# A graph attention kernel: a bank stretch set to zero by VectorE instead of by a product of zeros, and eleven unread products per layer taken out

## The reference

```python
xw = x @ W
xj = xw[src].reshape(-1, H, D) + edge_emb.reshape(-1, H, D)
alpha = einsum(xi, att_i) + einsum(xj, att_j)
alpha = leaky_relu(alpha, 0.2)
ea = exp(alpha - segment_max(alpha, dst)[dst])
alpha = ea / (segment_sum(ea, dst)[dst] + EPS)
aggr = segment_sum(xj * alpha[..., None], dst)
h = aggr.mean(axis=1) + b        # relu between the layers
```

## Time and profile before

| | us |
|---|---|
| median of three runs | 3877.42 |
| the three runs | 3877.04, 3877.42, 3886.52 |
| the profiled execution's own time | 3864.76 |
| its span, first to last instruction | 3862.7 |

### The profile page before, as it was taken

How to read it: one execution, slowest core, us unless ns; L and a number is a source line. 1 busy time by engine, 2 the same in 40 slices (tenths; PEclk the granted TensorE clock), 3 DMA queues, 4 the chain that set the end, 5 groups by cost and what they waited for, 6 DMA issues and landing times.

```text
span 3862.7 us, 48694 instructions
## 1 busy us (share of the span) xinstructions
PE 2537.2 (66%) x13702; PEld 2037.0 (53%) x13702; DVE 2037.4 (53%) x6415; ACT 700.5 (18%) x3102; POOL 2210.4 (57%) x2357
## 2 busy tenths in 40 slices
PE   7778726666592767659276765927676592767669
PEld 6668615555471555546165554716555471655556
DVE  8966635555462555546255554625454462555546
ACT  0067521111121111112111111221111122111111
POOL 0066566666626766661676666167676616766661
PEclk8555555555565555556555555665555566555556
DMA  3212022222202222220222222022222202222221
GB/s 105 87 58 78 18 61 51 52 52 57 51 19 50 54 52 52 56 48 18 49 54 50 54 57 50 18 49 54 50 54 57 50 18 49 54 50 54 52 47 34
DMA packets 114123, 195.78 MB, mean 51 GB/s; under 512 B 39897, under 2 KB 77272, under 8 KB 113864
## 3 DMA queue, kind: packets, MB, share of 16 engines
q0 software_dynamic: 62560, 130.25, 14.9%
q1 hardware_dynamic: 51304, 62.42, 5.1%
HBM read 180.86 MB, written 11.67 MB: 50 GB/s over the span
## 4 chain that ended last, share of the span: by engine, by line
PE 32%; DVE 32%; another core or an unknown queue 18%; issue 14%; DVEq 3%; ACT 1%; ACTq 1%; POOL 0%; DMA 0%; POOLq 0%
PE bank L736 13%; PE bank L738 7%; DVE acc L1200 3%; PE bank L744 3%; PE bank L709 2%; PE bank L732 2%; DVEq L1018 2%; DVE alpha L1094 2%; PE bank L781 2%; DVE pw L1161 2%; DVE into L1143 2%; PE bank L762 1%; DVE prod L1072 1%; DVE ring L849 1%
## 5 line engine op out<-in xcount | busy, mean ns | idle before, releaser
L509 POOL DMA_INDIRECT ring<-table,srci x1955 | 1937.5, 991 | 937.9 <-issue 556.7
L736 PE MATMUL bank<-pw,ring 128*128 128x48 f32 x3910 | 1216.1, 405 | 181.9 <-issue 179.7
L736 PEld LDWEIGHTS bank<-pw,ring 128*128 128x128 f32 x3910 | 1016.8, 315 | 330.9 <-issue 258.5
L1200 DVE TENSOR_TENSOR acc<-acc,bank 128x288 f32 x490 | 222.8, 455 | 1215.5 <-remote 830.0
L738 PE MATMUL bank<-onehot,est 128*36 128x24 f32 x3910 | 631.1, 243 | 203.5 <-issue 202.8
L732 PE MATMUL bank<-zeros 128*128 128x288 bf16 x490 | 210.6, 430 | 726.2 <-DVE pw L1161 485.5
L738 PEld LDWEIGHTS bank<-onehot,est 128*36 128x36 f32 x3910 | 390.8, 149 | 369.3 <-issue 200.5
L732 PEld LDWEIGHTS bank<-zeros 128*128 128x128 bf16 x490 | 58.4, 119 | 802.5 <-DVE pw L1161 501.2
L579 ACT COPY ai_win<-ai_rows 128x48 f32 x1955 | 339.5, 229 | 472.1 <-issue 436.8
L585 ACT ACTIVATE dd<-dd 128x66 f32<-128x66 f32 x75 | 19.4, 259 | 2171.5 <-DVE dd L1154 975.7
L516 POOL TENSOR_TENSOR S<-S 128x128 f32<-128x128 f32 x125 | 61.1, 489 | 399.8 <-ACT S L589 393.9
(11 more groups left out here) (213 smaller groups left out, 2773.0 us busy)
## 6 DMA issues: line engine op xcount, KB each, us to landing
ring<-table,srci POOLq DMA_INDIRECT x1955
ai_rows<-lo_dram SPq DMA_DIRECT2D x28, 896.0 KB, 4.3
at<-in_attr SPq DMA_DIRECT2D x65, 224.0 KB
table<-ring SPq DMA_DIRECT2D x15, 390.0 KB, 3.7
table<-ring SPq DMA_DIRECT2D x5, 325.0 KB, 3.2
result<-ring SPq DMA_DIRECT2D x24, 64.0 KB
x_mid<-ring SPq DMA_DIRECT2D x3, 384.0 KB, 2.7
table<-ring SPq DMA_DIRECT2D x5, 130.0 KB, 2.3
```

The source lines that it names most:

```text
L509: nc.gpsimd.indirect_dma_start(out=ring[:, slot(t), :], out_offset=None, in_=table, in_offset=bass.IndirectOffsetOnAxis(ap=srci[:, t:t + 1 ...
L736: nc.tensor.matmul(wide[:, 0:H, at_k], ring[:, slot(t), 0:D], pw[:, g % DEEP, k, :, :], start=False, stop=False, skip_group_check=True)
L1200: V.tensor_tensor(win, win, grp_sum(g).rearrange("p (r w) -> p r w", r=REG), ALU.add)\
```

## The change

VectorE sets a group's bank stretch to zero right after it has added it, when a group six further will use the bank (`g + DEEP < G`), and counts that in a new semaphore, `cleared`. The memset waits for its own add. TensorE waits for the count in place of multiplying zeros, except for the first six groups of a layer, which still use the product of zeros, since the banks were used for other things before. The `keep_warm` products are taken out, and with them the wait at the start of chunk 9 that kept them out of bank 3 while it was in use.

```diff
+        cleared = sem("cleared")
@@ aggregate
+                if g >= DEEP:
+                    pe.wait_ge(cleared, layer * (G - DEEP) + g - DEEP + 1)
                 pe.wait_ge(p_ready, gg + 1)
@@
-                nc.tensor.matmul(total, zeros[:, 0:P], zeros[:, :], start=True, stop=False, skip_group_check=True)
+                if g < DEEP:
+                    nc.tensor.matmul(total, zeros[:, 0:P], zeros[:, :], start=True, stop=False, skip_group_check=True)
@@
-            def keep_warm(times):
-                for _ in range(times):
-                    nc.tensor.matmul(bank[3][:, 0:21 * WIN], identf[:, :],
-                                     onehot[:, 0:21, :].rearrange("p t w -> p (t w)"), start=True, stop=True)
@@ the loop over a layer's groups
-                        if c == 9 and i == 0:
-                            pe.wait_ge(s_sb, n + NT)
-                        if c >= NC - 3 and i + 1 < len(GC[c]):
-                            keep_warm(1)
@@ add_group, after the add
+                if g + DEEP < G:
+                    v.wait_ge(added, layer * G + g + 1)
+                    V.memset(grp_sum(g), 0.0).then_inc(cleared, 1)
```

## The result

| | before | after |
|---|---|---|
| median of four runs, us | 3877.23 | 3828.56 |
| lowest to highest, us | 3874.46 to 3886.52 | 3818.19 to 3830.41 |
| the profiled execution's own time, us | 3864.76 | 3829.17 |

The ratio is 0.9861 with a 95% interval of 0.9844 to 0.9877: 48.7 us less by the medians, 54 us by the ratio. The forecast was 60 us less. After is therefore faster, and inside the range; the sizes of the single steps are what the experiments are for.

A forecast was written before the change was run, and what follows sets the result against it. The prediction took waits to bound chunks 0 to 11 and TensorE the last three chunks. Unread products -78, zero products -10 and memsets +28 gave -60 us: 3817 us from the median, range 3758 to 3886.

The forecast's parts named there:

- The unread products, 78 us: Last three chunks of each layer: taking out the keep_warm products gains 15.5 us per layer, 78 us in five.
- The two steps that asked what is late next: Chunk 12: 25 us, between TensorE's 23.5 and 26.8 with VectorE's chain; chunk 13: 17.6 us, VectorE the bound.
- The products of zeros, 10 us: Zero products removed from TensorE, 92 per layer: 10 us taken as the gain reaching the end.
- the bounds 0 to 42: Gain from removed zero products: 42 us in five layers if TensorE's sums were never held, 0 if nothing reaches the end.
- The memsets, 28 us: VectorE, from a chunk's last late sum to the next windows: one 0.47 us memset per chunk start, 28 us lost.
- The new wait on TensorE, nothing: TensorE's wait per group for a clearing made six groups earlier: always met, costed at nothing.
- a sign of being wrong: Profile after: TensorE waiting at its new wait for a clearing was listed among what would show the forecast wrong.
- The memsets decide: Rival: 187 of 460 uncovered memsets use up the gain; with 300 the kernel takes 3930 us; chance of slower 0.11.
- The clock: Rival: without keep_warm products the node products stay at 1.2 GHz, up to 125 us more, 3942 us; chance 0.04.
- The middle gains: Rival: sums in chunks 0 to 11 come earlier by 42 us, no memset uncovered, 3757 us; chance 0.10.
- What bounds the middle: Chunks 0 to 11: TensorE 66% busy, VectorE 51%, GpSimd 68%; no engine full, so waits decide.

The follow-up runs named there:

- the second memset: The changed kernel with a second memset of the same stretch behind each first one, which it waits for: 3845.94 us, ratio 0.9896.
- neither: The kernel before without keep_warm products, and with zero products only for a layer's first six groups, no memsets: 3778.28 us, ratio 0.9776.

## Why the prediction was right, point by point

**The unread products, 78 us: right, in size and mechanism.** The ends fall by 79.1 us over five layers, and the run with this part alone gives 80 to 83. Chunk 12 now takes 24.1 us in three of the layers and 25.1 in two (forecast 25), chunk 13 17.6 in four and 18.0 in one (17.6), chunk 14 9.9. The two steps that asked what is late next differ: in chunk 13 it is VectorE's chain, as the forecast had it; in chunk 12 it is mostly TensorE's own pace. Without memsets chunk 12 takes 23.9 us in three of the layers, and seven groups at the 3.41 us of the earlier trace rows are 23.9; with the memsets moved it takes 23.5 in four, the forecast's 7 x 3.36. That TensorE then waits for chunk 14's windows is in the timeline of after:

```profile
1776.12 0.62 DVE L1156 TENSOR_TENSOR pw<-onehot,est 128x192 f32<-128x192 f32 x2
```
```profile
1776.62 0.63 PE L740 MATMUL bank<-pw,ring 128*128 128x48 f32 x2 [4.15 <-DVE pw L1156]
```

**The products of zeros, 10 us: too large.** By the medians they were worth 0 to 3 us. The step that failed is the choice of 10 out of the bounds 0 to 42, "nearer to the part that the waits show". The argument in front of it (TensorE's work ends few of VectorE's waits in the middle) already led to the low end; the 10 was a share of work that had been found not to be on the way. Clear of the noise they counted only in the layer's end, where TensorE was the bound (13 us with the unread products kept), and the forecast has that under the unread products.

**The memsets, 28 us: right in size, in part by luck.** They cost 26 us with the products of zeros beside them, and 25 us come back when they are moved: the place in VectorE's queue counts, as the forecast had it. Its 0.30 us for a size that was not in the trace measured 298 ns. The 28 were 60 memsets at 0.47 us. In the trace of after a memset moves the next windows by 0.37 us, and 74 memsets lie between the last add that had waited for over 1 us and the next chunk's windows: 27 us. So the count was too small and the price too large, and they cancel. The kernel before has 112 such adds, which at 0.47 us would have been 53 us; taking one per chunk start was a choice, and it came out. That only these memsets are paid is argued, not shown: the second memset cost nothing in the middles, the gathers' length is a rival, and with the unread products kept the swap cost 13 us.

**The new wait on TensorE, nothing: right.** It was met at once but for 0.7 us in all, which as a wait was named a sign of being wrong, and as a cost is none. The wait at chunk 9 went with the unread products and was not tried alone.

**The sum.** Forecast -78 - 10 + 28 = -60. Measured by parts: -80 to -83, 0 to -3, +26 to +33 (33 is what the two chips' ratios give from neither to after, 0.9776 to 0.9861), and for the whole -49 to -54. The error of 6 to 11 us is about the 10 that the products of zeros didn't give.

**The rivals.** *The memsets decide* fell: 26 us are the price of 55 to 70 exposed ones, at 0.47 to 0.37 us each, where 187 were needed. *The clock* fell: the granted clock is 0.50 in the end and through the first 3.0 us of the node products, then 0.99, as in the earlier trace rows, although TensorE now waits 6 us of the 52.70 in the end. The Trainium skill, "TensorE: Matmul & The Clock Gate", section "Why this matters for your kernels", advises against such gaps; here a TensorE that was 99% busy had the low level, and lost nothing with the gaps. *The middle gains* fell: no run without the products of zeros gained there clear of the noise.

**What bounds the middle** was read too weakly. "No engine is full, so waits decide" is true of the shares, but the runs point to one source: GpSimd issues a gather every 1.25 us, 28 in a chunk are 35 us of the 40 that a chunk takes, and while they are issued the sums come late. It didn't change the sign, but it fits that TensorE's savings were worth next to nothing there: with all gathers TensorE's busy time is not what the chunk waits for.

## What to carry to other kernels

Work that goes from one engine to another is priced at its place in the other engine's queue. Here 460 memsets cost 26 us directly behind the adds and some 5 behind the next engine's input, so put such work behind that input. Work that is taken out gains only in the stretches where its engine is the bound; split the span by stretch first, and take the low end of the bounds elsewhere. When all engines are two thirds busy, ask which one issues at a fixed pitch: here half the gathers in four layers were worth some 785 us (ratios 0.9785 and 0.7760), the change itself 50.

## What the runs showed of the hardware

**A gather's cost is per instruction.** In layers 2 to 5 a gather lasts 990 ns on GpSimd for 128 rows of 130 numbers, 947 ns for 64 rows, and 996 ns for 26 numbers per row. A gather that fetches two tiles at once was not run. Beside VectorE's work it can last longer: in after the 525 gathers beside which no VectorE instruction ran lasted 946 ns on average and none over 1.1 us; of the other 1430, 276 did. Why is not shown.

**While gathers are issued, TensorE and ScalarE get their instructions slowly.** In after the same place as above, TensorE, then ScalarE, then GpSimd:

```profile
1305.06 0.24 PE L742 MATMUL bank<-onehot,est 128*36 128x24 f32 x1 [1.02 <-issue]
1307.19 0.20 PE L742 MATMUL bank<-onehot,est 128*36 128x24 f32 x1 [1.89 <-issue]
1309.30 0.24 PE L740 MATMUL bank<-pw,ring 128*128 128x48 f32 x1 [1.91 <-issue]
1312.11 0.24 PE L740 MATMUL bank<-pw,ring 128*128 128x48 f32 x1 [2.57 <-issue]
1314.22 0.20 PE L742 MATMUL bank<-onehot,est 128*36 128x24 f32 x1 [1.88 <-issue]
1315.66 0.20 PE L742 MATMUL bank<-onehot,est 128*36 128x24 f32 x1 [1.23 <-issue]
```
```profile
1311.42 0.23 ACT L580 COPY ai_win<-ai_rows 128x48 f32 x1 [1.17 <-issue]
1312.86 0.23 ACT L580 COPY ai_win<-ai_rows 128x48 f32 x1 [1.21 <-issue]
1314.26 0.23 ACT L580 COPY ai_win<-ai_rows 128x48 f32 x1 [1.16 <-issue]
```
```profile
1312.89 0.94 POOL L510 DMA_INDIRECT ring<-table,srci  x1 [0.30 <-issue]
1314.14 0.95 POOL L510 DMA_INDIRECT ring<-table,srci  x1 [0.30 <-issue]
...
1318.99 0.95 POOL L510 DMA_INDIRECT ring<-table,srci  x1 [2.65 <-remote]
```

From the first of these six instructions to the last 10.6 us pass, where four instructions of a tile take 0.84; both engines wait for nothing that the profile names, at steps of about 0.7 us or a multiple, and GpSimd issues at its full pitch until it waits itself. In the layers with half the gathers there are no such stretches: the four weight loads of a tile start within 0.9 us there, and up to 7.1 us apart in the first layer, with all gathers.

**Counts come late too.** The product at 1315.66 is the last of its sum, and VectorE's add waits until 1318.92. GpSimd's gather at 1318.99, which waits for a count of the same semaphore, starts with it. So it is the count that is late, and not VectorE alone. In the kernel before the same place shows it without slow products: the last one starts at 1312.27, the add at 1320.86, and a gather with it:

```profile
1320.93 0.95 POOL L509 DMA_INDIRECT ring<-table,srci  x1 [2.64 <-remote]
```

It isn't only TensorE's counts. The moved memset waits for nothing but counts that VectorE itself raises, and sat idle 86.5 us for what the profile doesn't name:

```profile
L1201 DVE MEMSET bank<- 128x288 f32 x460 | 137.1, 298 | 146.2 <-remote 86.5 <-issue 14.8 <-DVE maxes L1151 5.1
```

That the slow stretches and the late sums go with the number of gathers is shown; what passes between GpSimd and the other engines is not, and stays open.
